# The responses of a linear recurrence: one scan of 57 steps, or three scans of 19 steps joined by products

## The reference, cut to what matters

```python
A = softplus(p[..., 0]); dt = sigmoid(p[..., 1]); S = 1.0 / (1.0 + dt * dt * A)
bc = (v @ w_bc).reshape(Bsz, T, N_HEADS, 2, D_STATE)     # B and C, then normed
def step(carry, inp):
    z, xs = carry
    z = s * (z - d * a * xs + d * bu)
    xs = xs + d * z
    y = einsum('bhn,bhnp->bhp', Ct, xs)
```

## Time and profile before

| what | us |
|---|---|
| median of 3 runs | 1791.55 |
| lowest, highest | 1791.33, 1795.67 |
| the profiled execution | 1789.63 |
| its span in the trace | 1787.8 |

### The profile page before, as it was taken

The page is one execution under the profiler, slowest core; times in us unless marked ns, Lnnn a source line. Parts: engine busy times, 40 slices in busy tenths (PEclk is TensorE's granted clock), DMA queues, the critical chain, the costliest instruction groups (busy, mean ns, idle before and its releaser), DMA issues. The chain is left out here.

```text
span 1787.8 us, 36878 instructions
## 1 busy us (share of the span) xinstructions
PE 1481.6 (83%) x14394; PEld 1117.3 (62%) x14394; DVE 1304.5 (73%) x2822; ACT 1049.6 (59%) x1871; POOL 403.6 (23%) x420
## 2 busy tenths in 40 slices
PE   5899996886369879899999737996597999999795
PEld 5888986785256657664444627895486644446474
DVE  5988896599859656549996756885646379994566
ACT  6898896432278535456989215664202449995465
POOL 0000000000446430229940106874000310000200
PEclk9999998697679989897999858998698879999897
DMA  5110101000000010004520452221200000000101
GB/s 143 28 44 25 35 2 36 14 1 4 0 8 2 1 34 1 15 27 160 167 75 2 109 191 64 62 61 40 72 1 14 1 1 2 2 2 1 34 1 36
DMA packets 52751, 67.98 MB, mean 38 GB/s; under 512 B 11536, under 2 KB 41490, under 8 KB 52579
## 3 DMA queue, kind: packets, MB, share of 16 engines
q1 hardware_dynamic: 46022, 50.30, 9.2%
q0 software_dynamic: 3840, 9.18, 1.7%
q10 hardware_dynamic: 2716, 6.14, 1.4%
HBM read 46.97 MB, written 18.65 MB: 37 GB/s over the span
## 5 line engine op out<-in xcount | busy, mean ns | idle before, releaser
L2029 DVE TENSOR_REDUCE att_max<-banks 104x1 f32<-104x512 f32 (+1 forms) x480 | 296.2, 684 | 10.2 <-PE banks L1943 6.4
L2064 ACT ACTIVATE att_p<-banks 104x514 f32<-104x514 f32 (+1 forms) x480 | 262.2, 599 | 31.4 <-PE banks L1988 19.8
L339 PE MATMUL banks<-tok_wT,feature_halves 128*128 128x192 f16 x2592 | 228.3, 248 | 23.4 <-DVE feature_halves L365 12.2
L339 PEld LDWEIGHTS banks<-tok_wT,feature_halves 128*128 128x128 f16 x2592 | 216.1, 99 | 32.4 <-DVE feature_halves L365 18.0
L1988 PE MATMUL banks<-att_q,att_kT 64*104 64x257 f16 (+1 forms) x960 | 156.1, 300 | 3.1 <-ACT att_p L2064 2.5
L2004 PE MATMUL banks<-att_p,att_v 104*32 104x257 f32 (+1 forms) x1920 | 156.3, 397 | 1.3 <-ACT att_p L2064 0.6
L1943 PE MATMUL banks<-att_kT,att_q 64*104 64x512 f16 (+1 forms) x480 | 125.9, 423 | 5.6 <-DVE att_max L2029 3.1
L1988 PEld LDWEIGHTS banks<-att_q,att_kT 64*104 64x104 f16 (+1 forms) x960 | 62.0, 121 | 105.8 <-ACT att_p L2064 79.2
L365 DVE TENSOR_TENSOR feature_halves<-features,feature_halves 128x2048 f16<-128x2048 f32 x54 | 123.4, 2285 | 5.6 <-ACT feature_halves L462 5.6
L134 PE MATMUL banks<-ones 128*128 128x256 f16 x654 | 87.3, 291 | 28.5 <-PEq L251 13.8
L462 ACT CAST feature_halves<-features 128x2048 f16<-128x2048 f32 x54 | 102.2, 1893 | 10.0 <-PE banks L339 9.2
(11 more groups left out here) (463 smaller groups left out, 3447.9 us busy)
## 6 DMA issues: line engine op xcount, KB each, us to landing
expert_w_in<-in_L_ffn_w_dram SPq DMA_DIRECT2D x16, 576.0 KB, 4.4
expert_w_halves<-expert_w_halves SPq DMA_DIRECT2D x32, 288.0 KB, 2.7
tok_w<-in_L_tok_W_dram ACTq DMA_DIRECT2D x4, 1152.0 KB, 7.4
expert_w2s<-expert_w_halves SPq DMA_DIRECT2D x1, 4608.0 KB
expert_y<-expert_out SPq DMA_DIRECT2D x6, 513.0 KB
expert_w1s<-expert_w_halves SPq DMA_DIRECT2D x2, 1536.0 KB
raw<-in_x_dram SPq DMA_DIRECT2D x2, 1152.0 KB, 5.4
expert_w1s<-expert_w_halves SPq DMA_DIRECT2D x3, 768.0 KB
```

What stands on the lines that cost most here:

```text
L339: ins = pe.matmul(c.bank[t // 2][:, (t % 2) * D:(t % 2 + 1) * D], fh[:, s, q, z, t * 128:(t + 1) * 128], wT[:, y, k, 6 * q + wf, :], start ...
L2029: dve.reduce_max(mx[0:qn, n // NS % 2, 2 * gi + e, k:k + 1], bank_of(unit)[0:qn, 0:KEYS], X).then_inc(maxed, 1)
L2064: act.activation(p[0:kn, n % 4, :, :], c.pair[2 + n % 2][0:kn, :].rearrange("p (e q) -> p e q", e=2)[:, :, 0:HALF], ACT.Exp, scale=scale). ...
```

## The change

The responses are worked out in three blocks of SUB = 19 tokens side by side. A new table `block`, [108, y = 2, x = 6, l = 19, n = 21], holds z (y = 0) and x (y = 1) for the six pairs of half and block; it lies in `acT` behind `coef` and is zeroed by POOL in the block before. Each of 18 steps is two products and a sum over all six pairs and both z and x, which needs a fourth row of `coef`, S d d. Then block 0 is copied to `g`, POOL copies the diagonal parts of blocks 1 and 2, and DVE fills their columns left of the diagonal with products of a block's answers to its start values and the last row of the block before. POOL, not DVE, zeroes `g`. PE makes all products of B and C first, and turns `g` afterwards, as far as the semaphores `scanned`, `placed` and `joined` allow. Weights of B and C and D_skip are loaded in `mixer_project`, the weights to the place of `start_resp`.

```diff
-        coef = acT[:, 0, 0:2, :, :].rearrange("p s k t -> p (s k t)").rearrange("p (v q t) -> p v q t", v=3, q=2)
+        flat = acT.rearrange("p b s k t -> p (b s k t)")
+        coef = flat[:, 0:8 * L].rearrange("p (v q t) -> p v q t", v=4, q=2)
+        SUB = L // 3
+        block = flat[:, 8 * L:8 * L + 12 * SUB * (SUB + 2)].rearrange("p (y x l n) -> p y x l n", y=2, x=6, l=SUB)
...
+            @block_.sync
+            def _(sp):
+                sp.dma_start(wbc[:, :, :], c.ins["L0_attn_w_bc"].rearrange("(k p) n -> p k n", p=128)).then_inc(wbc_in, 16)
+                for e in range(2):
+                    for k in range(3):
...
+                sp.wait_ge(d_in, 96)
...
-                        pe.wait_ge(qs, 1)
-                        for q in range(3):
+                        pe.wait_ge(qs, 2)
+                        for q in range(4):
...
-                        own.did(dve.tensor_tensor(tmp[0:L, 1, :], S, dt, ALU.mult))
+                        own.did(dve.tensor_tensor(Sd, S, dt, ALU.mult))
                         own.wait()
-                        dve.scalar_tensor_tensor(q3[0:L, 2, :], tmp[0:L, 1, :], -1.0, A, ALU.mult,
-                                                 ALU.mult).then_inc(qs, 1)
+                        dve.scalar_tensor_tensor(q3[0:L, 0, :], Sd, -1.0, A, ALU.mult, ALU.mult).then_inc(qs, 1)
+                        dve.tensor_tensor(dt, Sd, dt, ALU.mult).then_inc(qs, 1)
...
-                                c.bank[6][0:LANES, 0:6 * L]).then_inc(pcopy, 1)
+                                c.bank[6][0:LANES, 0:8 * L]).then_inc(pcopy, 1)
+            @block_.gpsimd
+            def _(pool):
+                pool.memset(block[0:LANES].rearrange("p y x l n -> p (y x l n)"), 0.0).then_inc(cleared, 1)
...
+        @block_.gpsimd
+        def _(pool):
+            pool.memset(g[0:P].rearrange("p a b c -> p (a b c)"), 0.0).then_inc(zeroed, 1)
+            pool.wait_ge(zeroed, 1)
+            pool.wait_ge(scanned, 1)
+            for b in range(1, 3):
+                at = b * SUB
+                pool.tensor_copy(g[0:P, :, at:at + SUB, 2 + at:2 + at + SUB], xs[:, :, b, :, 2:BW]).then_inc(placed, 1)
...
         def _(dve):
             own = Own(dve, own_s)
-            own.did(dve.memset(g[0:P].rearrange("p a b c -> p (a b c)"), 0.0))
...
-            for t in range(L):
-                n = t + 3
...
+            flat = table.rearrange("p y x l n -> p y x (l n)")
+            own.did(dve.tensor_copy(flat[:, :, :, 2:2 + (SUB - 1) * (BW + 1) + 1:BW + 1], cf[:, 2:4, :, :]))
+            for z in range(2):
+                own.did(dve.tensor_copy(table[:, :, :, 0, z], cf[:, 1 - z:3 - z, :, 0]))
+            for t in range(1, SUB):
+                n = t + 2
+                shape = (P, 2, 6, n)
+                own.wait()
+                own.did(dve.tensor_tensor(from_x[:, :, :, 0:n], table[:, 1, :, t - 1, 0:n].unsqueeze(1).broadcast_to(shape),
+                                          cf[:, 0:2, :, t].unsqueeze(3).broadcast_to(shape), ALU.mult))
+                own.did(dve.tensor_tensor(from_z[:, :, :, 0:n], table[:, 0, :, t - 1, 0:n].unsqueeze(1).broadcast_to(shape),
+                                          cf[:, 1:3, :, t].unsqueeze(3).broadcast_to(shape), ALU.mult))
+                own.wait()
+                own.did(dve.tensor_tensor(table[:, :, :, t, 0:n], from_x[:, :, :, 0:n], from_z[:, :, :, 0:n], ALU.add))
             own.wait()
+            dve.wait_ge(zeroed, 1)
+            dve.tensor_copy(g[0:P, :, 0:SUB, 0:BW], xs[:, :, 0, :, :]).then_inc(scanned, 1)
+            for b in range(1, 3):
+                at, n = b * SUB, 2 + b * SUB
...
+                    dve.wait_ge(placed, 1)
+                    dve.wait_ge(joined, 1)
...
+                own.did(dve.tensor_tensor(dst, xs[:, :, b, :, 1].unsqueeze(3).broadcast_to(rows),
+                                          x_before.unsqueeze(2).broadcast_to(rows), ALU.mult))
+                own.did(dve.tensor_tensor(part, xs[:, :, b, :, 0].unsqueeze(3).broadcast_to(rows),
+                                          z_before.unsqueeze(2).broadcast_to(rows), ALU.mult))
...
+                own.wait(3)
+                dve.tensor_tensor(dst, dst, part, ALU.add).then_inc(joined, 1)
+                own.wait(1)
+                own.did(dve.tensor_tensor(zlast, zlast, zpart, ALU.add))
...
         def _(act):
+            for i in range(8):
+                act.wait_ge(done, i + 1)
+                act.copy(raw[0:L, bc_range(i)], c.bank[6 + i % 2][0:L, 0:per[i] * 96]).then_inc(moved, 1)
             for n, (q, t0) in enumerate(jobs):
...
         def _(pe):
             idn = c.const("ident", P)[:, 0:P]
+            pe.wait_ge(w_in, 16)
+            for i in range(8):
...
             for n, (q, t0) in enumerate(jobs):
...
-                pe.wait_ge(own_s, scan_count(t0 + k - 1))
+                ready = (t0 + k - 1) // SUB
+                pe.wait_ge(scanned, 1)
+                if ready:
+                    pe.wait_ge(placed, ready)
+                    pe.wait_ge(joined, ready)
```

More of the change, by code:

```diff
@@ L818, in _, with mixer_project @@
                 ins.then_inc(added, 1)
-def mixer_project(c, sg, vT, coef, win):
+def mixer_project(c, sg, vT, coef, block, win, wbc, wbc_in, dsk):
     nc = c.nc
@@ L834, in mixer_project @@
         qs, qt, silu = c.sem("lane_ready"), c.sem("lane_transposed"), c.sem("u_done")
+        cleared = c.sem("blocks_zeroed")
         jobs = [(g, m, b, s) for m in range(3) for b in range(BATCH) for s in range(3) for g in (1, 0)]
-        with nc.Block() as block:
-            @block.tensor
+        d_in = c.sem("D_skip_in")
+        with nc.Block() as block_:
+            @block_.sync
[3 more added lines that the diff above has]
+                    for k in range(3):
+                        h = 2 * k + e
+                        sp.dma_start(dsk[64 * e:64 * e + 64, k:k + 1], c.ins["L0_attn_D_skip"][h:h + 1].rearrange(
+                            "(a n) -> a n", a=1).broadcast_to((64, 1))).then_inc(d_in, 16)
+                sp.wait_ge(d_in, 96)
+            @block_.tensor
             def _(pe):
@@ L863, in _ @@
                         ins.then_inc(qt, 1)
-            @block.scalar
+            @block_.scalar
             def _(act):
@@ L887, in _ @@
                 silu_u(len(jobs) // 6 - 1)
-            @block.vector
+            @block_.vector
             def _(dve):
@@ L952, in mixer_responses @@
+def mixer_responses(c, ctx, coef, block, gs, ab, zx, de, vT, raw, w, w_in):
     nc = c.nc
     W = L + 2
+    SUB = L // 3
+    BW = SUB + 2
+    P = LANES
     g = c.sb(ctx, "G", [128, 2, L, W])
[L955 to L958, removed]
     r = c.xT[:, 0, 288:288 + 4 * NBC].rearrange("p (q v n) -> p q v n", q=2, v=4)
+    spare = c.xT.rearrange("p o n -> p (o n)")[0:P, 600:600 + 3000 - 600]
+    from_x, from_z = (spare[:, i * 12 * BW:(i + 1) * 12 * BW].rearrange("p (y x n) -> p y x n", y=2, x=6) for i in range(2))
+    zend = spare[:, 24 * BW:24 * BW + 4 * W].rearrange("p (i q n) -> p i q n", i=2, q=2)
+    second = spare[:, 800:800 + 2 * SUB * 2 * BW]
+    table = block[0:P]
+    zs, xs = (table[:, y].rearrange("p (q b) l n -> p q b l n", q=2) for y in range(2))
+    cf = coef[0:P].rearrange("p v q t -> p v (q t)").rearrange("p v (x l) -> p v x l", x=6)
@@ L960, in mixer_responses @@
     own_s, masked = c.sem("scan_steps"), c.sem("lane_masked_ready")
-    def scan_count(t):
-        return 8 + 6 * (t + 1)
+    zeroed, placed, joined = c.sem("G_zeroed"), c.sem("G_blocks_placed"), c.sem("G_blocks_joined")
+    scanned = c.sem("G_blocks_scanned")
     tp, ev, rest_ev = c.sem("G_transposed"), c.sem("G_copied"), c.sem("resp_copied")
-    P = LANES
     jobs = [(q, t0) for t0 in range(0, L, 4) for q in range(2)]
-    w = c.xT[:, 0, 0:288].rearrange("p (k n) -> p k n", k=3)
-    w_in, done, moved, d_in = c.sem("w_bc_in"), c.sem("bc_done"), c.sem("bc_moved"), c.sem("D_skip_in")
+    done, moved = c.sem("bc_done"), c.sem("bc_moved")
@@ L1004, in _ @@
-            own.wait()
-            def prev(q, t):
-                return g[0:P, q, t - 1, 0:t + 3] if t else x0[0:P, 0:3]
-            for t in range(L):
-                n = t + 3
[L1011 to L1023, removed]
@@ L1027, in _ @@
+            own.wait()
+            dve.wait_ge(joined, 2)
+            dve.wait_ge(placed, 2)
+            for q in range(2):
+                vals = [zend[:, 0, q, 0:1], g[0:P, q, L - 1, 1:2], g[0:P, q, L - 1, 0:1], zend[:, 0, q, 1:2]]
                 for j, v in enumerate(vals):
@@ L1042, in _ @@
                          c.bank[n % 6][0:L, 0:k * P].rearrange("p (a b) -> p b a", a=k)).then_inc(ev, 1)
[L1043 to L1048, removed]
+        @block_.tensor
         def _(pe):
             idn = c.const("ident", P)[:, 0:P]
+            pe.wait_ge(w_in, 16)
+            for i in range(8):
+                if i >= 2:
+                    pe.wait_ge(moved, i - 1)
+                for j in range(per[i]):
+                    at = (5 * i + j) * L
```

(4 more changed lines are left out.)

42 lines of the change are left out of this document (23 added, 19 removed).

## The result

In the first comparison the changed kernel took 1766.2 us (median of 4 runs, 1761.87 to 1768.64) against 1791.49 of before: ratio 0.9865, 95% interval 0.984 to 0.989. With two later comparisons of the same pair it is 1766.04 us in 14 runs, 1758.85 to 1771.49, and before, in all comparisons on several chips, 1791.5 us in 74 runs, 1782.02 to 1801.65. The forecast was 1763.3 us, range 1758 to 1771. The runs of one kernel spread over 13 us (after) and 20 us (before), far more than the executions showed on which the forecast stood. Much of that goes with the clock of PE: of the 70 executions of before whose mean granted clock is on record, the ten fastest had 0.894 to 0.901 of full speed and the ten slowest 0.884 to 0.890.

What follows compares the result with a forecast made beforehand. The prediction took DVE's serial scan as the bound: 15.6 us replacing 55.4, then joins, ACT's copies and tail, ending the stage at 442.7 instead of 471.06. That 28.3 us off the median 1791.55 gave 1763.3 us, range 1758 to 1771.

Steps and rivals of the forecast that it cites:

- What bounds the stage: Stage from 401 to 471 us: one serial chain on DVE, a memset of 5.66 us and 57 scan steps.
- The block before and the move of the loads: Block before the stage: one more DVE product costs 0.3 us; turnings, POOL's memset and the moved loads cost nothing.
- The lock on the first copy: Stage start: DVE's first three copies wait for POOL's memset until 407.7 us, the scan starts at 408.3.
- rival A: Stage start: copies don't wait for the memset; stage ends at 439.9, 31.1 us gained, time 1760.4 us; chance 0.2.
- The scan: DVE's new scan takes 15.6 us in place of 55.4 and ends at 423.9.
- rival C: DVE's broadcast and strided four-dimensional views cost a multiple per element, making the kernel slower, 1797 us at 3.3 ns; chance 0.02.
- Rival B: DVE's chain costs more: scan up to 4.1 us, POOL's copies 0.8 or more; time 1768.5 to 1770.5 us; chance 0.2.
- The copy and the joins: DVE after the scan: 9.6 us plus 0.8 us for POOL's copies, last join at 434.3 us.
- PE's products: PE beside the scan: products from 402.0 take 21.1 us, until 423.1; PE then waits 1.8 us for block 0.
- ACT and the tail: Stage end: ACT's copies 0.47 us apart, last ends at 440.1; tail 2.6 us at full clock; end at 442.7.
- Two signs that were named for being wrong: Within the stage: joins stretched by POOL's copies, and the clock at half during PE's turnings, would speak against the forecast.
- The sum: Whole stage: ends at 442.7 instead of 471.06, 28.3 us gained, 1763.3 us against the median; nothing changes behind it.

Runs made afterwards that it cites:

- e2: Kernel before with its old scan, only PE's and ACT's order changed to products of B and C first; median 1793.7 us, ratio 1.0004.
- e3: Changed kernel with the old order, one group of products after every third job of turnings; median 1790.5 us, ratio to before 0.9994.
- e0: The changed kernel run again without any edit; median of four runs 1766.81 us.
- e1: Changed kernel with POOL's memset of g placed behind DVE's first three copies; median 1762.28 us, ratio to before 0.9835.
- e8: The changed kernel run a third time without any edit; median 1763.9 us in 6 runs, ratio to before 0.9836.

## Why the prediction was right, step by step

- *What bounds the stage.* Right: e2 shows that PE's and ACT's order is no bound beside the scan, and e3 that a shorter scan shortens the stage.
- *The block before and the move of the loads.* No cost seen; DVE's copy took 0.63 us for 0.51, under ACT's silu as said. The stage began 0.9 us sooner in this execution and 0.8 us later in e0's (ACT's last silu at 399.87 and 401.57), so the 0.3 us can't be read from it.
- *The lock on the first copy* (DVE waits until POOL's memset is through). Right, and the largest single choice: rival A (chance 0.2) would have had the copy free. The copy took 5.5 us more than in e1. It met the memset otherwise than forecast: both started at the head of the stage, at 400.77 and 400.81, and not the copy at 403.4 in the middle of it; the end of the wait is the same. e1 is rival A built on purpose: its stage ends at 437.85, where A had 439.9.
- *The scan.* 15.6 us forecast, 15.95 measured (406.82 to 422.77). The cost per element and the gaps carried over to strided, four-dimensional views, which disposes of rival C. Rival B's upper bound for the scan, 4.1 us more, did not come.
- *The copy and the joins.* The first product of the joins started 0.49 us behind the copy's start, not 0.9; POOL's copies were 1.46 us each, not 0.8, and stretched the joins by 1.2 us, not 0.8. By luck the errors cancel: 10.5 us from the copy's start to the last join's end against 10.4 forecast.
- *PE's products.* 19.65 us against 21.1: the clock was at half for 3.4 us and not for 4.8. The products ended at 420.46, and PE then waited 3.0 us for the copy of block 0 where 1.8 was forecast; DVE held the path, so this error cost nothing.
- *ACT and the tail.* Twelve jobs in 5.11 us against 5.24; the tail 2.8 us at the full clock against 2.6. The forecast's claim that ACT and DVE hold the end nearly alike is seen in PE's two short waits for the joins, 2.9 us in all. Two signs that were named for being wrong did come, at a small price: POOL's copies stretched the joins, and in e0's and e8's profiles the clock was at half for 3.4 us during the turnings, at lengths of 42.3 and 42.6 us.
- *The sum.* 28.3 us forecast, 28.2 measured as length. The sentence that does not hold as it stands is "Behind the stage nothing changes". The work did not change, but its time is not fixed: the later loss is 1.8 to 10.9 us in three profiles of the changed kernel, and 0 and 9.8 us in two of the kernel before. The level from which the forecast took its 28.3 us, the median of 1791.55, was sound: 74 runs have 1791.5. The 2.7 us between 1763.3 and the 1766.04 of 14 runs are gain of the stage that is missing in the medians; they are within the intervals, and no run shows which part they belong to. The executions of before that were known ahead of the forecast lay within 6.1 us (1789.63 to 1795.67), where 74 spread over 20. So they did not show this uncertainty, but the range of 13 us held it.

## What to carry to other kernels

Ask of a shortened chain what had been hidden beneath it: here the shorter scan by itself was worth 10 us of stage and the reordering by itself nothing, and together they were worth 28. When a fill (a memset) moves from DVE to POOL, look at what DVE does beside it: here a plain copy waited until the fill ended, and products with two inputs didn't. Putting the copies in front made the stage 4 us shorter; that the whole time follows is not shown. And measure a change of one stage by the stage's own length in several profiles: whole times of one and the same kernel here spread over 13 to 20 us.

## What was not expected of the hardware

The granted clock of PE in a part 500 us behind the change is at half for 20.5 us or not at all. It was at half in 7 of 14 profiles, once in two of the kernel before and once in three of the changed kernel, and cost 5.8 to 6.1 us. A DVE copy of 228 elements took 5.93 us beside a POOL memset of 5.70 us, and 0.42 us in front of it. A DVE product of 42 elements took 0.79 us beside POOL's copy and 0.20 us without.
